# A graph network in one launch: attention's mask in bf16, and two loaded counts bounded by a bitwise and

## What is computed

```python
x = layernorm(x + L0(x))     # two transformer convolutions, 4 heads of 64
x = layernorm(x + L1(x))     # three relational layers

# one transformer convolution
q, k, v = x @ wq + bq, x @ wk + bk, x @ wv + bv
alpha = (q[dst] * k[src]).sum(-1) / sqrt(64)      # softmax over each node's edges
out = segment_sum(softmax(alpha) * v[src], dst) + x @ ws + bs   # then batch norm, leaky relu

# one relational layer
msg = relu(x[src] * (edge_attr @ nn_w.T + nn_b))
out = x @ root + bias + sum(mean_of(msg where type == r, dst) @ W[r] for r in range(3))
```

## Time and profile before

| | |
|---|---|
| median of three runs | 4121.45 us (4115.07 to 4121.66) |
| span of the profiled execution | 4117.9 us |
| sort, tables, projections | 0 to 640 us |
| attention, layer 0 | 640 to 1290 us |
| attention, layer 1 | 1390 to 2075 us |
| relational layers | 2148 to 2720, 2785 to 3370, 3425 to 4040 us |
| busy over the span | PE 75%, PEld 57%, DVE 70%, ACT 37%, POOL 66% |

### The profile page before, as it was taken

The page is one execution under the profiler, slowest core; times in us unless marked ns, Lnnn a source line. Parts: engine busy times, 40 slices in busy tenths (PEclk is TensorE's granted clock), DMA queues, the critical chain, the costliest instruction groups (busy, mean ns, idle before and its releaser), DMA issues.

```text
span 4117.9 us, 112272 instructions
## 1 busy us (share of the span) xinstructions
PE 3104.7 (75%) x28301; PEld 2331.3 (57%) x28301; DVE 2876.4 (70%) x10466; ACT 1533.8 (37%) x4045; POOL 2706.7 (66%) x2886
## 2 busy tenths in 40 slices
PE   6886027777776987777648888897888888888887
PEld 4443015555554565555436666676666667666666
DVE  9998026777776677777667777766777766777777
ACT  1000006777764267777623333212333321333320
POOL 5777747777774377777647777636777745777760
PEclk8777558999998999999969999899999989999988
DMA  3222157888884578888834444314443323444430
GB/s 77 55 57 48 27 162 218 237 237 236 237 230 84 162 228 238 237 237 236 200 108 124 123 120 120 108 58 125 122 120 115 114 73 90 122 119 117 116 105 32
DMA packets 386267, 574.01 MB, mean 139 GB/s; under 512 B 134783, under 2 KB 272433, under 8 KB 386163
## 3 DMA queue, kind: packets, MB, share of 16 engines
q0 software_dynamic: 155264, 442.19, 37.8%
q1 hardware_dynamic: 176106, 123.76, 10.1%
q10 hardware_dynamic: 54794, 6.81, 1.1%
HBM read 531.37 MB, written 41.08 MB: 139 GB/s over the span
## 4 chain that ended last, share of the span: by engine, by line
PE 19%; issue 19%; DVE 16%; DVEq 10%; DMA 10%; POOL 7%; ACT 2%; ACTq 1%; POOLq 0%; SPq 0%
DMA ht<-kv_rows,gidx 6%; PE bank L1210 6%; DVE region L1873 6%; DVEq L728 4%; PE bank L1049 3%; POOL ht L584 3%; PE bank L1197 3%; DVE rings L1854 3%; DMA gring<-kv_rows,gidx 2%; DVE rings L1860 2%; POOL gring L618 2%; PE bank L1124 2%; POOL gring L584 2%; PE bank L1145 2%; PE bank L1157 1%
## 5 line engine op out<-in xcount | busy, mean ns | idle before, releaser
L618 POOL DMA_INDIRECT gring<-h_rows,gidx x1248 | 1201.1, 962 | 464.3 <-issue 317.2
L1210 PE MATMUL bank<-rings 128*128 128x96 f32 x6168 | 914.8, 297 | 247.2 <-DVE region L1873 245.3
L1210 PEld LDWEIGHTS bank<-rings 128*128 128x128 f32 x6168 | 811.0, 205 | 444.8 <-DVE region L1873 406.8
L1281 ACT ACTIVATE rings<-rings 128x512 f32<-128x512 f32 x771 | 485.6, 630 | 1366.2 <-DVE rings L1854 1313.0
L1854 DVE TENSOR_TENSOR rings<-bank,gring 128x256 f32<-128x256 f32 x1542 | 582.4, 420 | 390.1 <-PE bank L1210 195.2
L584 POOL DMA_INDIRECT gring<-kv_rows,gidx x512 | 485.7, 949 | 245.9 <-issue 133.4
L1873 DVE TENSOR_TENSOR region<-region,bank 128x192 f32 x1542 | 540.0, 350 | 131.8 <-PE bank L1210 14.7
L584 POOL DMA_INDIRECT ht<-kv_rows,gidx x512 | 486.2, 950 | 173.7 <-issue 118.4
L1322 ACT ACTIVATE ht<-ht,ntop 128x129 f32<-128x129 f32 x1024 | 413.8, 404 | 287.0 <-DVE ntop L1788 278.4
L1197 PE MATMUL bank<-nnwt,rings 64*128 64x256 f32 x3084 | 491.0, 442 | 39.1 <-DMA rings<-edge_attr_T 39.1
L559 POOL DMA_INDIRECT edge_records<-rings x416 | 408.3, 981 | 151.3 <-issue 148.5
(11 more groups left out here) (257 smaller groups left out, 4095.4 us busy)
## 6 DMA issues: line engine op xcount, KB each, us to landing
rings<-node_in_window_T SPq DMA_DIRECT2D x256, 128.0 KB
rings<-edge_attr_T SPq DMA_DIRECT2D x1548, 16.0 KB
gring<-h_rows,gidx POOLq DMA_INDIRECT x1248
kv_rows<-rows SPq DMA_DIRECT2D x50, 258.0 KB, 2.5
rows<-h_rows SPq DMA_DIRECT2D x75, 128.0 KB
gring<-kv_rows,gidx POOLq DMA_INDIRECT x512
ht<-kv_rows,gidx POOLq DMA_INDIRECT x512
region<-edge_records SPq DMA_DIRECT2D x13, 576.0 KB, 7.0
```

Of the source, the lines that this page charges most:

```text
L618: g.indirect_dma_start(out=gring_r[:, 2 * u + k, :], out_offset=None, in_=h_d[l], in_offset=bass.IndirectOffsetOnAxis(ap=gidx_r[:, half, 2 ...
L1210: ins = pe.matmul(b[:, (2 * k + c) * SEG:(2 * k + c + 1) * SEG], prod[:, slot % RL, (2 * k + c) * P:(2 * k + c + 1) * P], one, start=True, ...
L1281: act.activation(prod[:, slot % RL, :], prod[:, slot % RL, :], ACT.Relu).then_inc(s_msg, 1)
```

## The change

The mask of attention is written by L1831, and read by L1788, as bf16 in place of fp32; its space in `rings` is halved. Where a count that was loaded from the job tables is the value of a wait, a bitwise and is taken of it first: with 511 for POOL's count of jobs (at most 257), with 255 for DVE's count of landed gathers (at most 208). No value changes by it.

```diff
+FREEMASK, LANDMASK = 511, 255
@@
-        mask = ring_space(2 * Q * P).rearrange("p (h t e) -> p h t e", h=2, t=Q)
+        mask = ring_space(Q * P).bitcast(BF16).rearrange("p (h t e) -> p h t e", h=2, t=Q)
@@ relation_gathers, POOL
-                        freed = g.snap(free_regs[u], min_val=1, max_val=RPAIRS)
+                        freed = g.snap(free_regs[u], min_val=1, max_val=RPAIRS) & FREEMASK
                         g.wait_ge(s_prod, freed + l * RPAIRS)
                         g.wait_ge(s_sp, freed + l * RPAIRS)
@@ job_registers, DVE
             def landed(slot):
-                return eng.snap(sets[slot // (U // 2)][2 * HALF + slot % (U // 2)], min_val=1, max_val=GPAIRS)
+                return eng.snap(sets[slot // (U // 2)][2 * HALF + slot % (U // 2)], min_val=1, max_val=GPAIRS) & LANDMASK
```

## The result

The changed kernel takes 4202.61 us (4201.63 to 4204.49, 4 runs), the kernel before in the same comparison 4119.31 us (4115.07 to 4121.66, 4 runs). The ratio is 1.0205 (1.019 to 1.0219), 83 us slower. The forecast was 4125 us, in a range from 4111 to 4137.

What follows compares the result with a forecast made beforehand. Gathers were taken to bound attention, and DVE's queue to lead the relational layers. DVE's and +4.0, POOL's and 0, mask written -0.5, mask read 0 gave +3.5 us on 4121.45: 4125 us, range 4111 to 4137.

Steps and rivals of the forecast that it cites:

- Attention: Attention layers: gathers 1.25 us apart set the time and hide the mask's saving; only -0.5 us on the span.
- 355 was worked out: Mask instruction L1831 in attention: 355 ns in bf16 instead of 486, taking half of its column part.
- 33.5 were forecast: DVE in attention: 33.5 us less busy from 256 masks, each 0.13 us shorter.
- the third rival: Attention: a shorter mask lets POOL's gathers run freer, 9 us if all of it goes, 4112 us; chance 0.08.
- POOL's and at nothing: POOL's queue: 600 ands, 3.6 us in all, hidden by the gather before and costed at 0.
- The queue on the path of the relational layers: Relational layers: DVE's queue decides when a pair begins; 65% of an added operation's time is paid.
- a path of more or less than 65%: Sign of a wrong prediction: the relational layers' path passes through DVE's queue less or more than 65%.
- the 6.2 us: DVE's queue time for the ands: 771 at 8 ns each, before taking 65% of it.
- The step that failed: DVE's landed count: the and fuses with its neighbours as the addition does, 8 ns each.
- The rival that came true: DVE's queue: each and is a separate instruction of 0.09 us; +45 us, 4166 us, at full price 4190; chance 0.12.
- 51 or 52: Expected ns of the fused copy, and and addition at L737 in layers 1 and 2.
- +4: Relational layers: cost of DVE's ands, 6.2 us x 0.65 = +4.0 us, bounds 0 and +6.2.

Runs made afterwards that it cites:

- e9: Changed kernel with the mask back in fp32, both ands kept, on a chip of usual speed: 4208.78 us, ratio 1.0203 to the kernel before.
- e1: Changed kernel with the mask back in fp32, both ands kept, on the slower chip: 5075.94 us, ratio 1.0064 to the kernel before there.
- e4: Changed kernel with both ands replaced by maxima with 1, mask in bf16, on the slower chip: 5029.04 us, ratio 0.9977 to the kernel before.
- e6: Changed kernel with POOL's and replaced by a maximum with 1, DVE's and kept: 4204.99 us, ratio 1.0208 to the kernel before.
- e7: Changed kernel with DVE's and taken after the addition, so copy and addition stay neighbours: 4165.75 us, ratio 1.0116 to the kernel before.
- e8: Changed kernel with DVE's and taken twice, with 511 and with 255: 4248.59 us, ratio 1.0314 to the kernel before.
- e10: Changed kernel with both ands replaced by maxima with 1, mask in bf16, on a usual-speed chip: 4134.38 us, ratio 1.0023 to the kernel before.
- e5: Changed kernel with DVE's and replaced by a maximum with 1, POOL's and kept: 4131.94 us, ratio 1.0032 to the kernel before.
- e12: Changed kernel with maxima for the ands, DVE's count worked out a pair earlier and its register loads moved earlier: 4059.0 us, ratio 0.984.
- e11: Changed kernel, ands kept, with DVE's count worked out one pair earlier for three of four pairs: 4112.48 us, ratio 0.9976.

## Why the prediction was wrong

**Attention, right on this chip.** L1832 takes 353 ns where 355 was worked out, and L1789 has the same median of 351 ns with either mask (means 349 and 350). The groups of DVE between 640 and 2075 us have 128.9 us for the masks before and 96.9 after, 32.0 less where 33.5 were forecast. The other groups there took some 8 us more (L1788 and its read of the accumulator 2.3, L1798 1.4, L1775 1.1, two copies 3.0), which nothing of the change explains, and instructions overlap at their ends, so the three windows of attention show DVE only 8.5 + 2.6 + 8.7 = 20 us less busy. The stages keep their length, and e9 confirms it with a ratio equal to that of the changed kernel. The gathers run no freer, 949 ns before and after: the third rival, and the rule of the Trainium skill that stood beside it (SBUF — State Buffer, "SBUF: two separate sides"), would have given a gain here; 32 us less of the mask gave none. That the gathers hide the mask holds where they lead: on the chip of e1 to e4, where POOL waits for its buffers, attention was 12 to 15 us shorter with the bf16 mask.

**POOL's and at nothing, right.** e6 without it is as slow as the changed kernel. It did part the copy from the addition there too, and the gather before covers that as well.

**The queue on the path of the relational layers, right in kind and too low in share.** I took 65% of an operation's time as paid. Measured are 0.063 us for each operation, of 0.07 to 0.08 us that one adds between L1874 and L1855 (0.38 - 0.30, and 0.45 - 0.38), so some 80 to 90%. The prediction named a path of more or less than 65% as a sign of being wrong, and by that sign this term failed too. On the 6.2 us that it was applied to, it would have moved the forecast by 1 to 2 us only.

**The step that failed** reads: "The and has the same neighbours as that addition, so I take it that it joins them." It does not join; e7 and e8 with their 771 and 2056 lone ALU_OPs show it, and that the time follows them. (The description of the kernel before says that operations next to each other appear as one `FUSED_REGOPS`; that is so for copies, additions and maxima, and not for the bitwise and.) The row that I had for a pair of neighbours was of a copy and an addition, and I carried it over to another operation. This made 6.2 us of queue time out of 1285 x 0.07 to 0.08 = 90 to 103 us.

**The rival that came true was too small.** "The and is an instruction of its own" was priced at 771 x 0.09 us and 65%, 4166 us. It left out that an instruction between copy and addition unfuses those: 514 more of them. With 1285 at its own 0.09 x 0.65 it gives 75 us, 4197, close to the 4203 measured, and e7, in which only the and stands alone, came to 4166. That closeness is in part luck: 0.09 us was too much for an operation (0.07 to 0.08) and 65% too little of it, and the two make 0.059, near the 0.063 measured.

**Even an operation that fuses was priced too low.** 8 ns held beside a lone copy (e10, layer 0) but not beside copy and addition: 26 ns, a FUSED_REGOPS of 70 ns where the prediction had 51 or 52. Such a change of the counts costs +10 to +12 us (e5, e10), where I had +4.

**What stays open.** PE's granted clock in the relational layers fell from 0.93 and 0.90 to 0.89 and 0.87, and stands at 0.95 to 0.96 in e12, where PE's idle time before this sum over the edges is 222 us against 281 in the changed kernel. The slower the queue, the lower the clock: the mean matmul of L1210 takes 297 ns before, 304 after and 289 in e12. No run parts the clock from the queue. The short steps between pairs, where little but the queue has room, hold 71 of the 84.4 us, so on balance some 13 us are left for the clock and everything else. Of e12, too, only the sum is known: it is 53 us under e11 on the same chip, by the moved loads and the maxima together.

## What to carry to other kernels

A register operation between two engine instructions has the price of its place: ask whether the engine waits anyway there, and count the operations that stay lone instructions, those included that the new one parts. Where an engine of middling busy share leads the chain with "issue" between its pieces, move its queue's copies, sums and loads behind an instruction that the queue waits out in any case; here that turned a ratio of 1.0205 into 0.9976 with every and still made, and with the loads moved as well into 0.984. Take the price of an edit from a row of that same operation, and where there is none, let the range reach to the unfused case.

## What the runs showed of the hardware

A bitwise and on a count is an ALU_OP of 45 ns (40 to 50) on DVE's queue and of 35 ns on POOL's, never part of a `FUSED_REGOPS`, while a maximum and an addition join a copy. On DVE, a copy alone takes 36 ns, with an addition or a maximum 44, with both 70.

One chip ran the kernel before in 5041 us, others in 4119 to 4124, and every stage is longer on it: the first attention layer takes 856 us in e4 and 651 in e10, the same kernel on another chip, the first relational layer 694 and 565. In e4 PE sat idle before the values' matmul (L1147), without a releaser that the trace shows, for 643.7 us, 809 times; in e10 for 84.8 us, 300 times. The DMA rate in attention was lower too (175 GB/s in e4). What lies behind it was not found.
